# Gate and up products of two token tiles as seven block products of mixed operands, in one pass over pairs of tiles

## The reference

```
h2  = layernorm(x1) * (1 + scale_b) + shift_b          # per batch
g, u = h2 @ w_gate, h2 @ w_up                          # 512 -> 2048
hid = silu(g) * u                                      # in each group of 4 the two
hid = hid * mask(the 2 largest |hid| of each group)    # largest magnitudes stay
out = x1 + gate_b * (hid @ w_down)                     # 2048 -> 512
```

## Time and profile before

| | |
|---|---|
| median of 3 runs | 1441.78 us (1441.34 to 1442.45) |
| the profiled execution | 1442.22 us, its span 1440.4 us |
| PE, DVE, ACT, POOL busy | 97%, 61%, 35%, 38% |
| matmuls | 6866, of them 4608 of phase B |
| first and last matmul of phase B | at 353.8 and 1434.3 us |
| DMA queues, share of 16 engines | 18.9% |

### The profile page before, as it was taken

One profiled execution on the slowest core, in us unless ns is written; L12 is line 12 of the kernel. 1 busy time (PEld: TensorE's weight loads), 2 busy tenths in 40 slices (PEclk: granted clock), 3 DMA queues, 4 the chain that ended last, 5 costly groups with the idle time before them and its releaser, 6 DMA issues.

```text
span 1440.4 us, 18863 instructions
## 1 busy us (share of the span) xinstructions
PE 1394.2 (97%) x6866; PEld 1139.9 (79%) x6866; DVE 881.5 (61%) x1260; ACT 507.4 (35%) x793; POOL 547.2 (38%) x367
## 2 busy tenths in 40 slices
PE   8999999998989999999999999999999999999997
PEld 4588888887768888888888887778888888888885
DVE  6777777778575636555555657574645555463654
ACT  5466666665622222122122233332222212222211
POOL 1755665666053313131332334462313223231311
PEclk9999999999999999999999999999999999999999
...
GB/s 242 117 31 117 66 80 87 87 58 125 168 89 7 96 0 95 11 84 61 33 66 29 124 29 95 88 124 1 95 25 69 66 29 69 26 95 0 66 0 95
DMA packets 23657, 102.41 MB, mean 71 GB/s; under 512 B 2629, under 2 KB 3141, under 8 KB 13901
## 3 DMA queue, kind: packets, MB, share of 16 engines
q1 hardware_dynamic: 23628, 102.05, 18.9%
...
...
## 4 chain that ended last, share of the span: by engine, by line
PE 78%; DVE 12%; issue 4%; ACT 3%; DMA 1%; POOL 1%; DVEq 0%; SPq 0%; ACTq 0%
PE bank L1111 25%; PE bank L1113 24%; PE bank L1112 24%; DVE banks_r L936 2%; PE bank L1132 1%; PE bank L1182 1%; DVE h_abs L1063 1%; PE bank L1120 1%; DVE one_each L1051 1%; DMA wmod_sb<-in_wmod_dram 1%; DVE x_ring L899 1%; DVE combT_lo L905 1%; PE bank L1192 1%; DVE pair_lo L1045 1%; DVE ln_raw L767 1%
## 5 line engine op out<-in xcount | busy, mean ns | idle before, releaser
L1026 DVE TENSOR_TENSOR h_act<-bank,silu_g 128x512 f32<-128x512 f32 x128 | 88.1, 690 | 408.8 <-PE bank L1113 388.1
L451 POOL TENSOR_TENSOR hs_lo<-h_abs,hs_hi 128x512 fp32r<-128x512 f32 x128 | 174.7, 1395 | 417.6 <-ACT hs_hi L671 417.6
L403 POOL TENSOR_TENSOR h_lo<-h_raw,h_hi 128x512 fp32r<-128x512 f32 x64 | 125.1, 1983 | 238.8 <-ACT h_hi L654 238.8
L1111 PE MATMUL bank<-h_hi,up_w_hi 128*128 128x512 f32 x512 | 200.7, 392 | 7.7 <-DVE h_act L1026 6.0
L1111 PE MATMUL bank<-h_hi,gate_w_hi 128*128 128x512 f32 x512 | 200.6, 392 | 7.3 <-ACT silu_g L677 4.5
L1111 PE MATMUL bank<-down_w_hi,hs_hi 128*128 128x512 f32 x512 | 200.1, 391 | 2.4 <-POOL hs_lo L451 2.4
L1112 PE MATMUL bank<-h_lo,up_w_hi 128*128 128x512 f32 x512 | 200.0, 391 | 0.0
L1113 PE MATMUL bank<-h_hi,up_w_lo 128*128 128x512 f32 x512 | 199.9, 390 | 0.0
L1112 PE MATMUL bank<-h_lo,gate_w_hi 128*128 128x512 f32 x512 | 199.9, 390 | 0.0
L1112 PE MATMUL bank<-down_w_lo,hs_hi 128*128 128x512 f32 x512 | 199.9, 390 | 0.0
L1113 PE MATMUL bank<-h_hi,gate_w_lo 128*128 128x512 f32 x512 | 199.9, 390 | 0.0
...
## 6 DMA issues: line engine op xcount, KB each, us to landing
h_raw<-h2T_scratch SPq DMA_DIRECT2D x16, 1024.0 KB, 4.8
x_ring<-in_x_dram SPq DMA_DIRECT2D x8, 1024.0 KB, 4.9
x_scratch<-x_ring SPq DMA_DIRECT2D x8, 1024.0 KB, 3.9
h2T_scratch<-h_full SPq DMA_DIRECT2D x8, 1024.0 KB, 3.9
over_x<-x_scratch SPq DMA_DIRECT2D x8, 1024.0 KB, 4.9
acc_scratch<-over_x SPq DMA_DIRECT2D x8, 1024.0 KB, 3.9
over_x<-acc_scratch SPq DMA_DIRECT2D x8, 1024.0 KB, 4.8
out_dram<-over_x SPq DMA_DIRECT2D x8, 1024.0 KB, 3.9
```

What stands on the lines that cost most here:

```text
L403: nc.gpsimd.tensor_tensor(h2_lo[:, k], h2_raw[:, k], h2_hi[:, k].bitcast(F32), ALU.subtract).then_inc(h2_lo_done, 1)
L451: nc.gpsimd.tensor_tensor(hs_lo[:, j], h_abs[:, j], hs_hi[:, j].bitcast(F32), ALU.subtract).then_inc(hs_lo_done, 1)
L1026: nc.vector.tensor_tensor(h_act[:, cc, j], bank[2 * (j % 2) + 1][:], silu_g[:, j % 2], ALU.mult).then_inc(h_done, 1)
L1111: nc.tensor.matmul(out_, stat[0], mov[0], start=start, stop=False)
```

## The change

Phase B goes once over 4 pairs of tiles. Both tiles of a pair (side a and side b) need gate and up, and each product sums over 2 halves of the 512 channels. Channel half x side on one hand and channel half x (gate, up) on the other make a 2 x 2 by 2 x 2 block product. It is done with seven products instead of eight: P1, P2, P5, P6, P7, P4, P3, each of 6 matmuls, on sums and differences of the blocks. A unit `u` is 128 hidden channels (16 per pair, hidden chunk c = u // 4, j = u % 4), 42 matmuls instead of 48. P1, P6, P7 and P4 share a bank that keeps on summing; between them ACT copies its state out (`keep1` L820, `keep2` L827, `keep3` L834), and DVE adds these copies into the gate and up of both sides. The down product has 48 matmuls per side and chunk, as before, in two banks in turn; DVE adds each to `y`. The work on hidden values (silu, magnitudes, mask, `hs_high`, `hs_low`) stays the same in kind and count.

The mixed operands are made in rounds: SP loads 4 raw blocks into one of two buffers `mix`, POOL makes 4 sums (`mix_comb`), ACT the high halves of 7 operands (`mix_high`, 128x896), POOL the low halves (`mix_low`), SP stores both to DRAM. There are 32 rounds for the weights (W, made once) and 8 per pair for the activations (A). 2 more rounds (D) per item bring the down weights and split them anew for each pair. 18 W and A rounds run in phase A (2 per tile, 4 in the last), the others at a step (`AT_STEP`): in the first pair 2 W rounds per step for u = 0 to 10, then A rounds 3, 3 and 2; in pairs 1 and 2 one A round per step for u = 4 to 11; 2 D rounds wherever j = 0 (except in the very first step). POOL issues the loads of mixed weights (`load_unit`, 768 KB and 1024 KB per unit, two units in the ring) and of mixed activations (`load_act`, 7 x 1024 KB per pair, one buffer). POOL also takes over multiplying by the gate row and adding x1 (`finish`, at steps 2 to 5 of the next pair), with x1 read in pieces of 256 KB into one buffer. Weights resident in SBUF, `split_w`, `acc_scratch`, and loading and splitting h2 in phase B are gone. The core of the diff:

```diff
...
 SA, CA, GA, SB, CB, GB = range(6)
...
+        def unit_steps(u, last):
+            if last and u == UNITS - 1:
+                return [(u, P6), (u, P7), (u, P4), (u, P3)]
+            return [(u, P6), (u + 1, P1), (u, P7), (u + 1, P2), (u, P4), (u + 1, P5), (u, P3)]
+        FINISH = {2: (0, 1, 2), 3: (3,), 4: (4, 5), 5: (6, 7)}
...
+        AT_STEP = {}
+        for p in range(NP):
+            plan = [weight_rounds(u) for u in range(5, UNITS)] if p == 0 else [[]] * (ACT_STEP - 1)
+            acts_left = act_rounds(p + 1) if p + 1 < NP else []
+            for u in range(UNITS):
+                c, j = divmod(u, J)
+                item = CHUNKS * p + c - 1
+                here = [("D", item, half) for half in range(2)] if j == 0 and item >= 0 else []
+                if u < len(plan):
+                    here += plan[u]
+                else:
+                    take = 3 if p == 0 else 1
+                    here += acts_left[:take]
+                    acts_left = acts_left[take:]
+                AT_STEP[p, u] = list(range(len(ROUNDS), len(ROUNDS) + len(here)))
+                ROUNDS += here
+        LAST = len(ROUNDS)
...
+            def mix_load(r):
+                par, spec = r % 2, ROUNDS[r]
+                if r >= 2:
+                    if ROUNDS[r - 2][0] == "D":
+                        sp.wait_ge(wd_lo_done, SPLIT[r - 2] + 1)
+                    else:
+                        sp.wait_ge(mix_lo_out[par], 16 * STORED[r])
...
+            def mix_store(r):
+                par, spec = r % 2, ROUNDS[r]
...
+                sp.wait_ge(mix_hi_done, MIXED[r] + 1)
+                sp.dma_start(to[:, :, 0], mix_hi[:].bitcast(F32)).then_inc(mix_hi_out, 16)
+                sp.wait_ge(mix_lo_done, MIXED[r] + 1)
+                sp.dma_start(to[:, :, 1], mix[par][:, 0:OPS]).then_inc(mix_lo_out[par], 16)
...
+            def load_x1(p, block_):
+                side, s = divmod(block_, S)
+                sp.dma_start(x1_piece[:], x1_t[SIDES * p + side][:, s]).then_inc(x1_in, 16)
+            def store_y(p, block_):
+                side, s = divmod(block_, S)
+                sp.wait_ge(y_done, 2 * S * p + block_ + 1)
+                sp.dma_start(out_t[SIDES * p + side][:, s], y[:, side, s]).then_inc(y_out, 16)
...
+            def rounds_of(p, u):
+                for r in AT_STEP[p, u]:
+                    if r > len(IN_TILES) and ROUNDS[r][0] == "D":
+                        mix_load(r)
+                    if r + 1 < LAST and ROUNDS[r + 1][0] != "D":
+                        mix_load(r + 1)
+                    mix_store(r)
...
+            def mix_comb(r):
...
+                pool.wait_ge(mix_in[par], LOADED[r] + 48)
+                if kind == "W":
+                    nc.gpsimd.tensor_tensor(e[P5], e[OPS], e[P4], ALU.add).then_inc(mix_step, 1)
+                    nc.gpsimd.tensor_tensor(e[P7], e[P1], e[OPS], ALU.subtract).then_inc(mix_step, 1)
+                    pool.wait_ge(mix_step, at + 2)
+                    nc.gpsimd.tensor_tensor(e[P6], e[P5], e[P1], ALU.subtract).then_inc(mix_step, 1)
+                    pool.wait_ge(mix_step, at + 3)
+                    nc.gpsimd.tensor_tensor(e[P3], e[P2], e[P6], ALU.subtract).then_inc(mix_step, 1)
...
+            def mix_low(r):
+                par, spec = r % 2, ROUNDS[r]
+                if spec[0] == "D":
...
+                    return
...
+                pool.wait_ge(mix_hi_done, MIXED[r] + 1)
+                nc.gpsimd.tensor_tensor(ops.bitcast(F32R), ops, mix_hi[:].bitcast(F32), ALU.subtract).then_inc(mix_lo_done, 1)
...
+            def finish(p, block_):
+                side, s = divmod(block_, S)
+                i = 2 * S * p + block_
+                if block_ == 0:
+                    pool.wait_ge(gb_in, 16 * (p + 1))
+                pool.wait_ge(y_added, 2 * S * (CHUNKS * p + CHUNKS - 1) + block_ + 1)
+                nc.gpsimd.tensor_tensor(y[:, side, s], y[:, side, s], gb_row[:], ALU.mult).then_inc(y_scaled, 1)
+                pool.wait_ge(x1_in, 16 * (i + 1))
+                pool.wait_ge(y_scaled, i + 1)
+                nc.gpsimd.tensor_tensor(y[:, side, s], y[:, side, s], x1_piece[:], ALU.add).then_inc(y_done, 1)
...
+            def pair(p):
+                first, last = p == 0, p == NP - 1
+                for u in range(UNITS):
+                    c, j = divmod(u, J)
+                    m, cp = CHUNKS * p + c - 1, (c - 1) % CHUNKS
+                    side, jj = divmod(j, 2)
+                    rounds = AT_STEP[p, u]
+                    if rounds:
+                        mix_comb(rounds[0])
+                    if m >= 0 and side == 1:
+                        hs_low(m, cp, side, 2 * jj)
+                        hs_low(m, cp, side, 2 * jj + 1)
+                    for i, r in enumerate(rounds):
+                        mix_low(r)
+                        if i + 1 < len(rounds):
+                            mix_comb(rounds[i + 1])
+                    if m >= 0 and side == 0:
+                        hs_low(m, cp, side, 2 * jj)
+                        hs_low(m, cp, side, 2 * jj + 1)
+                    for block_ in FINISH.get(u, ()) if p else ():
+                        finish(p - 1, block_)
+                    for unit, o in unit_steps(u, last):
+                        n = UNITS * p + unit
+                        if unit == UNITS - 1 and not last:
+                            pool.wait_ge(p_done[o], n + 1)
+                            load_act(p + 1, o)
+                        if o in (P5, P3) and not (last and unit + 2 >= UNITS):
+                            pool.wait_ge(p_done[o], n + 1)
+                            load_unit((unit + 2) % UNITS, int(o == P3), first=first and unit + 2 < UNITS)
...
+            for p in range(NP):
+                pair(p)
+            m = ITEMS - 1
+            for r in (LAST, LAST + 1):
+                mix_low(r)
+            for side in range(SIDES):
                 for j in range(J):
...
+            def mix_high(r):
+                par, spec = r % 2, ROUNDS[r]
...
+                at = MIXED[r]
+                act.wait_ge(mix_step, 4 * at + 4)
+                if at:
+                    act.wait_ge(mix_lo_done, at)
+                    act.wait_ge(mix_hi_out, 16 * at)
+                nc.scalar.activation(mix_hi[:], mix[par][:, 0:OPS], ACT.Copy).then_inc(mix_hi_done, 1)
...
+            def keep2(p, u, first=False):
+                n = UNITS * p + u
+                act.wait_ge(p_done[P6], n + 1)
+                if not (first and u < 2):
+                    act.wait_ge(gate_b_sum, n - 1)
+                nc.scalar.activation(keep_u2[:, u % 2], bank_of(u, 0), ACT.Copy).then_inc(u2_kept, 1)
...
+                first, last = p == 0, p == NP - 1
+                for u in range(UNITS):
+                    c, j = divmod(u, J)
+                    m = CHUNKS * p + c
+                    mp, cp = m - 1, (c - 1) % CHUNKS
+                    rounds = list(AT_STEP[p, u])
+                    end = last and u == UNITS - 1
+                    keep2(p, u, first)
+                    if j % 2 == 1:
+                        silu_of_b(p, u - 1)
+                    if not end:
+                        keep1(p, u + 1, first)
...
+                    keep3(p, u, first)
...
+                        hs_high(mp, cp, j // 2, 2)
+                    if rounds:
+                        mix_high(rounds.pop(0))
...
+                    if mp >= 0 and j == 0:
+                        if mp == 0:
+                            act.wait_ge(x1_out, 16 * NT)
+                        hs_high(mp, cp, 0, 0, first=mp == 0)
+                        hs_high(mp, cp, 0, 1)
+                        absolute(mp, cp, 1, 0)
+                        absolute(mp, cp, 1, 1)
+                    elif mp >= 0 and j == 1:
+                        hs_high(mp, cp, 0, 3)
+                        absolute(mp, cp, 1, 2)
...
+                    elif mp >= 0:
+                        hs_high(mp, cp, 1, 3)
+                    for r in rounds:
+                        mix_high(r)
+                    if j == 3:
+                        for jj in range(3):
+                            absolute(m, c, 0, jj, first=m == 0)
+                    if j % 2 == 1:
+                        silu_of_b(p, u)
+                    if j == 3:
+                        absolute(m, c, 0, 3)
...
+            BANK = {P1: 0, P6: 0, P7: 0, P4: 0, P2: 1, P5: 2, P3: 2}
+            BEGINS = (P1, P2, P5)
...
+            def product(p, u, o, first=False):
+                n, par = UNITS * p + u, u % 2
+                pe.wait_ge(w_in[int(o >= 3)][par], 16 * (UNITS // 2 * p + u // 2 + 1))
+                if u % UNITS == 0:
+                    pe.wait_ge(act_in[o], 16 * (p + u // UNITS + 1))
...
+                    pe.wait_ge(p1_kept, n + 1)
+                elif o == P7:
+                    pe.wait_ge(u2_kept, n + 1)
+                elif o == P4:
+                    pe.wait_ge(u3_kept, n + 1)
+                elif o == P3:
```

(17 more changed lines are left out.)

921 lines of the change are left out of this document (492 added, 429 removed).

## The result

The changed kernel takes 1712.22 us (median of 4 runs, 1711.83 to 1712.72) against 1442.12 us beside it: a ratio of 1.187, with a 95% interval of 1.186 to 1.189. The profiled execution has a span of 1710.9 us. So it became slower, as forecast, but by 270 us instead of 118, and past the end of the range.

The account below looks back on a forecast made before the run. The prediction took PE, busy 97% of the span, as the bound. From 1440.4 us it removed 86.9, 8.5 and 11.8 (1333.2), added 225 of stalls and clock (1558.2) and 1.8 around the span: 1560 us, range 1390 to 1650.

Parts of the forecast that it names:

- the 20.3 that I took out: Old kernel's waits expected to go: 8.5 us at the change of pass and 11.8 at phase B's start.
- phase A: Two rounds in each of 7 tiles stall PE 1 us per tile: +7 us (0 to 21).
- last tile and hand-over: POOL's four rounds and 11 DMA issues, and loads waiting for stores, stall PE: +16 us (6 to 30).
- pair 0, down windows with it: Pair 0's rounds delay copies and `hs_lo`, +76 us (60 to 105); DVE overfills down windows, +6 (0 to 20).
- pairs 1 and 2: A and D rounds, `finish` and the boundary stall PE 30 us in each: +60 us (30 to 90).
- pair 3: PE stalls at steps u = 2 and u = 4: +10 us (4 to 16).
- tail: Side a's `finish` stands ahead of side b's `hs_lo` on POOL, then the last four blocks: +20 us (10 to 24).
- clock: Matmuls slow after long waits; some 20 stalls at 1.5 us each: +30 us (15 to 60).
- Removed: Six of 48 matmuls gone in each of 64 units: 384 at 0.2263 us, 86.9 us saved.
- Price of a round: A comb, high, low chain takes about 5.0 us, 3.9 of them POOL's; `mix_low` 2.08, `wd_lo` 2.35, ACT's high halves 0.94.
- The rounds hide: Faster rival: helpers' slack covers the rounds, all stalls total 62 us, time 1397 us; chance 0.22.
- Port contention: Slower rival: POOL slows DVE's two-input work, 4 us more in some 28 down windows, +112: 1672 us; chance 0.10.

Follow-up runs that it names:

- 2: Changed kernel without the weight and activation rounds inside the four pairs, loads reading earlier operands (output not the reference's): 1513.7 us.
- 3: Changed kernel with POOL's `hs_low` for side a right behind the first round's low half, or before it in a half's second step: 1697.8 us.
- 5: Changed kernel whose W and A rounds in the pairs load and store nothing but keep POOL's and ACT's work (output not the reference's): 1663.4 us.
- 9: Changed kernel with side b's last silu and the magnitudes ahead of the second and third `mix_high` on ACT at odd j: 1693.2 us.
- 10: Changed kernel with 3 and 9, and from u = 4 in pair 0 mostly one round at even j, three at odd j; pairs 1, 2 re-dealt: 1649.7 us.
- 1: Changed kernel with pair 0's seven activation loads spread over the last tile's four subtiles instead of all at the first: 1718.1 us.
- 6: Changed kernel with attention's last sums and ring loads before POOL's last two rounds, and `combT_high` before them on ACT, at the hand-over: 1708.5 us.
- 11: Changed kernel with 3, 6, 9, 10, early down-weight loads, tail x1 pieces preloaded with `hs_low` before `finish`, and `finish` spread behind ring loads: 1608.1 us.

## Why the prediction was wrong

The direction was right, and so was its mechanism: PE waits by the order of the queues, at copies on ACT behind `mix_hi` and at `hs_lo` behind rounds (runs 2, 3, 5, 9, 10). The sum was mis-sized: it put 225 us for all that was added, and took pair 0, the clock, the hand-over and the tail too small. PE's idle time is 304 us in all, where I had said some 190. Up to the last tile's wait for `combT_lo` the changed kernel needs 354.63 us where the kernel before needed 339.44: 15.2 more. From there to the end it needs 1356.3 against 1101.0, with 86.9 us fewer of matmuls: 342.2 more. With the 20.3 that I took out, 377.7 stand where I had put 225. Term by term, by PE's idle times added up:

| term | forecast | measured |
|---|---|---|
| phase A | 7 (0 to 21) | 15.2 |
| last tile and hand-over | 16 (6 to 30) | 32.9 (47.25 against 14.36 us) |
| pair 0, down windows with it | 76 + 6 | 132.1 |
| pairs 1 and 2 | 60 | 64.3 |
| pair 3 | 10 | 13.6 |
| tail | 20 | about 43 |
| clock (measured: pairs only) | 30 | about 82 |

The measured ones add to 383, 5 more than the difference. Most of that lies in what I took out: of the 234 matmuls that I priced at 0.2263 at the start of phase B before, 28 are transposes, 3.2 us in all, so some 12 us were lost there and not 8.2.

**Removed.** 384 matmuls gone, as said. The 0.2263 us of each holds at full clock: from 414.38 to 419.82 us the changed kernel starts 24 of them in 5.44 us.

**Price of a round.** Right: `mix_low` 2.07 us (2.08), the sums 0.45 each (0.44), `wd_lo` 2.35 (2.35), `mix_hi` 0.95 (0.94). These are the durations with nothing beside them; the means are 2.15 for `mix_low` and 2.45 for `wd_lo`. A ring load's issue on POOL took 0.56 us (0.35 to 1).

**Pair 0.** The single places were within 7 us each: after u = 4 15.0 us and 10.8 (9 and 9), after u = 8 9.1 and 10.3 (9 and 9), after u = 12 15.7 and 10.3 (17 and 8.5), u = 6 and 10 4.2 each (4), u = 7 9.0 (5), u = 11 3.7 and 12.0 (9), the boundary 4.6 (4.6). The step that failed is "POOL catches up in the downs after them, so I take +76": it does not. The list came to 96, and nothing of it was caught up: of the 50 us that are missing (132 against 76 + 6), 20 are this share, and the rest are places priced too low. Run 9 shows why for the odd steps: a late round holds ACT, ACT holds the silu, DVE holds `y`, and PE stops inside the down product that was to be the cover. Chunk 0 cost 20 us in waits of over 1.5 instead of 8. There is no down product there, and the store of a round's low half can take a whole step to land, here in the chain that ended last of the changed kernel:

```profile
429.74 10.65 DMA wmix_scratch<-mix
...
448.71 11.13 DMA wmix_scratch<-mix
...
467.96 10.23 DMA wmix_scratch<-mix
```

I had taken about 3 us for a store, and 4.3 is the median; but each of these three was issued within 0.5 us of two ring loads of POOL (at 429.66, 448.62 and 467.69 us, and 0.6 later), which took 5.6 to 9.7 us themselves. Run 5 puts the transfers of all rounds in the pairs at 49 us.

**Hand-over.** I counted POOL's rounds and 11 issues, but took a store for 3.9 us as in the earlier trace rows. With the DMA engines full it took up to 20.4, and a round's buffer comes free only then (runs 1 and 6).

**Pairs 1 and 2, pair 3.** Right within 4.3 and 3.6 us, and the places too: 6.8, 5.1, 9.2 and 4.0 us in pair 1; only `hs_lo` after u = 8 cost 0.8 there where I had 4.5.

**The clock.** "20 x 1.5 = +30" is the second step that failed. I took the loss after waits of 2.2 and 6.0 us as 1.4 and 3.4 and then used the small one for most. There are 25 waits of 4 us or more in pairs 0 to 3 alone, 12 of them in pair 0, of which eight are 9 to 16 us long. They follow so closely in pair 0 that its mean granted clock is 0.81, against 0.96 in pair 3. Taking idle time and 0.2263 per matmul from a pair's length leaves 44, 16, 13 and 9 us for pairs 0 to 3 (for pair 0 with 918 large matmuls, and less 3 of transposes). It is a cost of the waits, not beside them: in run 2 the clock is 0.97.

**Tail.** The x1 chain was seen, at 4.6 us a block (4.7 to 6.1 by the trace). I let some of it lie beside the down product; it lay ahead of `hs_lo` (14.86 us of waiting), and the same chain ran once more for side b: the end comes 17.5 us after the start of the last matmul, 6.1 before. From 1625 on 146 matmuls worth 33.0 take 85.9, with 27.2 us of waiting and a mean clock of 0.71, against some 10 beyond their worth at the end of the kernel before.

**The rivals.** "The rounds hide" (1397) is refuted by 2 and 5: they cost 198 us. Port contention gave 1672, nearest to the measured time, and that is luck: contention is there, but in sum no larger than before. The groups of the changed kernel:

```profile
L1231 DVE TENSOR_TENSOR first_wins<-h_abs 128x1024 bf16<-128x1024 f32 x32 | 48.3, 1509 | 0.0
L1229 DVE TENSOR_TENSOR pair_lo<-h_abs 128x1024 f32<-128x1024 f32 x32 | 43.3, 1352 | 5.6 <-ACT h_abs L848 5.6
L1259 DVE TENSOR_TENSOR hidden<-pair_lo,hidden 128x512 f32<-128x512 bf16 x128 | 126.5, 1010 | 1.1
```

The same two in the kernel before, and its last multiplication by the mask:

```profile
L1046 DVE TENSOR_TENSOR first_wins<-h_abs 128x1024 bf16<-128x1024 f32 x32 | 59.8, 1868 | 0.0
L1045 DVE TENSOR_TENSOR pair_lo<-h_abs 128x1024 f32<-128x1024 f32 x32 | 55.5, 1736 | 0.0
L1063 DVE TENSOR_TENSOR h_abs<-keep,h_act 128x512 f32<-128x512 bf16 x128 | 99.7, 841 | 1.1
```

`pair_lo` takes 1352 ns in the mean, against 1.22 us undisturbed and 1736 ns in the mean before; 4 of 32 take over 2.0 us. Only the last multiplication is slower than before, 1010 against 841 ns. Against the shortest duration of each form, DVE lost 17.5 us in pair 0 and 70 us in all from 401.88 us on, where the kernel before lost 117 in phase B with PE at 97%; POOL lost 13.1 and 50, against 37. PE waited for `y` twice in pair 0, both times with DVE idle, and run 9 removed both by a move on ACT. The rule of the Trainium skill, "SBUF — State Buffer", section "Who interferes with whom", does show here: 9 of 32 `first_wins` take 2.03 to 2.29 us, and beside one of them, at 534.90 us, two `hs_lo` took 4.45 us where two took 2.54 at 517.12:

```profile
517.12 2.54 POOL L571 TENSOR_TENSOR hs_lo<-hidden,hs_hi 128x512 fp32r<-128x512 f32 x2
...
533.85 4.45 POOL L571 TENSOR_TENSOR hs_lo<-hidden,hs_hi 128x512 fp32r<-128x512 f32 x2
```

That is about 1 us of the wait of 10.76. It explains none of the two waits for `y`. No run takes contention away alone, so its share of PE's waits is not measured; the runs that only move work (3, 9, 10 and 11) show that order is worth up to 104 us.

**Left open.** What of phase A's 15 us is POOL's two rounds per tile and what their traffic wasn't tried. Nor was a second `mix_hi` buffer, which would let ACT go on while a round's low half is made and stored.
